# Value products of an attention stage: eight heads in two slots of a step in place of four heads in four

## The reference, cut to what matters

```python
scores = jnp.einsum('bhqd,bhkd->bhqk', q, k) / jnp.sqrt(jnp.asarray(D, q.dtype))
attn = jax.nn.softmax(scores, axis=-1)
out = jnp.einsum('bhqk,bhkd->bhqd', attn, v)
out = out.transpose(0, 2, 1, 3).reshape(B, N, C)
return out @ Wo.T + bo
```

## Time and profile before

| | |
|---|---|
| median of 3 runs | 976.9 us (973.17 to 978.64) |
| the profiled execution, its own time | 973.87 us |
| its span, first to last instruction | 972.1 us |
| TensorE busy with matmuls | 805.2 us, 83% |
| VectorE busy | 594.3 us, 61% |
| ScalarE busy | 404.9 us, 42% |
| GpSimd busy | 356.3 us, 37% |
| mean granted TensorE clock | 0.918 of full |
| L757 (value products) | 1024 records, 73.8 us busy |

### The profile page before, as it was taken

How to read it: one execution, slowest core, us unless ns; L and a number is a source line. 1 busy time by engine, 2 the same in 40 slices (tenths; PEclk the granted TensorE clock), 3 DMA queues, 4 the chain that set the end, 5 groups by cost and what they waited for, 6 DMA issues and landing times. The chain is left out here.

```text
span 972.1 us, 16867 instructions
## 1 busy us (share of the span) xinstructions
PE 805.2 (83%) x5933; PEld 635.1 (65%) x5933; DVE 594.3 (61%) x1410; ACT 404.9 (42%) x639; POOL 356.3 (37%) x290
## 2 busy tenths in 40 slices
PE   5999955568998888899888887885299999999993
PEld 4777734345666666666656665543299999999993
DVE  4879854444578776777877766643255555555542
ACT  4565621123555554455455545551243233423320
POOL 0333434212254444455354444223222344235422
PEclk9999988767999999999999999875599999999997
DMA  4116401553554454464455434100533332233100
GB/s 121 44 45 201 131 19 60 127 136 94 125 132 130 114 156 136 125 157 119 115 136 157 130 111 131 55 21 21 177 96 101 115 108 98 91 114 120 38 27 18
DMA packets 75913, 100.91 MB, mean 104 GB/s; under 512 B 10961, under 2 KB 63354, under 8 KB 75856
## 3 DMA queue, kind: packets, MB, share of 16 engines
q1 hardware_dynamic: 72400, 92.03, 34.0%
q0 software_dynamic: 3456, 8.13, 2.3%
HBM read 65.47 MB, written 35.74 MB: 104 GB/s over the span
## 5 line engine op out<-in xcount | busy, mean ns | idle before, releaser
L971 DVE TENSOR_REDUCE nmax<-ps_m 128x4 f32<-128x1024 f32 x128 | 156.7, 1224 | 117.5 <-PE ps_m L732 114.7
L925 ACT ACTIVATE pt<-ps_a 128x1024 f32<-128x1024 f32 x128 | 131.1, 1024 | 138.0 <-PE ps_a L742 136.6
L1238 ACT ACTIVATE hid<-ps_h 128x640 fp32r<-128x640 f32 x64 | 45.1, 705 | 151.3 <-PE ps_h L1178 151.3
L1178 PE MATMUL ps_h<-xt,w_hi 128*128 128x320 f32 x512 | 100.0, 318 | 1.0 <-DVE xt L1253 1.0
L732 PE MATMUL ps_m<-kst,qst 48*128 48x256 f32 x512 | 68.7, 349 | 33.7 <-DMA qst<-halves_dram 30.1
L732 PEld LDWEIGHTS ps_m<-kst,qst 48*128 48x128 f32 x512 | 41.2, 199 | 77.8 <-issue 35.6
L1287 DVE SCALAR_TENSOR_TENSOR hid<-ps_h,hid 128x640 fp32r<-128x640 f32 x64 | 52.8, 825 | 56.1 <-ACT hid L1238 55.6
L1190 PE MATMUL ps_y<-w_hi,hid 128*128 128x256 f32 x640 | 85.3, 284 | 1.7 <-issue 1.7
L1178 PEld LDWEIGHTS ps_h<-xt,w_hi 128*128 128x128 f32 x512 | 80.1, 191 | 5.5 <-DVE hid L1287 3.3
L1190 PEld LDWEIGHTS ps_y<-w_hi,hid 128*128 128x128 f32 x640 | 80.1, 191 | 1.9 <-issue 1.9
L166 POOL TENSOR_TENSOR gated<-xh,sgate 128x512 f32<-128x512 f32 x32 | 42.2, 1319 | 88.1 <-ACT xh L259 88.1
(11 more groups left out here) (169 smaller groups left out, 1623.9 us busy)
## 6 DMA issues: line engine op xcount, KB each, us to landing
halves_dram<-half SPq DMA_DIRECT2D x64, 256.0 KB, 2.5
gated<-in_w SPq DMA_DIRECT2D x16, 1024.0 KB, 5.5
kst<-halves_dram SPq DMA_DIRECT2D x64, 128.0 KB, 3.2
qst<-halves_dram SPq DMA_DIRECT2D x64, 128.0 KB, 3.2
rows_dram<-blank SPq DMA_DIRECT2D x1, 5160.0 KB, 19.2
gated<-rows_dram SPq DMA_DIRECT2D x8, 645.0 KB, 4.2
x_raw<-in_x_t SPq DMA_DIRECT2D x8, 512.0 KB, 3.8
xres<-in_x SPq DMA_DIRECT2D x16, 256.0 KB, 3.8
```

Source lines behind the costliest of these rows:

```text
L925: nc.scalar.activation(pt[:, k % 4].rearrange("p s t q -> p (s t q)"), ps_a[:].rearrange("p s t q -> p (s t q)"), ACT.Exp).then_inc(s["exp ...
L971: nc.vector.tensor_reduce(nmax[:, q, :, :, h // 2].rearrange("p t s -> p s t"), ps_m[:], AX.X, ALU.max, negate=True).then_inc(s["max_done" ...
L1178: mm = pe.matmul(ps_h[:, f % 2, c2, 0:HC], w1[a][:, p, k, f * P:(f + 1) * P], xt[:, b, p, k, c2 * HC:(c2 + 1) * HC], start=(n == 0 and k = ...
L1238: nc.scalar.activation(hid[:, HI, f, :].rearrange("p (c n) -> p c n", c=2), ps_h[:, f % 2, :, 0:HC], ACT.Relu).then_inc(s["hid_hi"], 1)
```

## The change

`weigh` is no longer called at h = 0 and h = 8. At h = 4 and h = 12 it is called twice, for groups g-1 and g: 16 matmuls in place of 8. The number of matmuls and their operands are the same. `pt` has one buffer for each of the 8 pairs of a batch, and ScalarE's wait ahead of an exponential names the value products of the same pair in the batch before.

```diff
-    pt = T("pt", [P, 4, 2, KT, S], F32)
+    pt = T("pt", [P, NP, 2, KT, S], F32)
...
-                                       pt[:, h // 2 % 4, h % 2, t, :],
+                                       pt[:, h // 2, h % 2, t, :],
...
-                    if head % PV == PV - 1 and on(n, lag):
+                    if head % (2 * PV) == 2 * PV - 1 and on(n, lag):
+                        weigh(j, p if lag == 2 else q, head // PV - 1)
                         weigh(j, p if lag == 2 else q, head // PV)
...
-                        need(act, s["pv_mm"], NG4 * j + k // 2 - 1)
-                        nc.scalar.activation(pt[:, k % 4].rearrange("p s t q -> p (s t q)"),
+                        need(act, s["pv_mm"], NG4 * j + k // 2 + 1 - NG4)
+                        nc.scalar.activation(pt[:, k].rearrange("p s t q -> p (s t q)"),
```

## The result

The changed kernel takes 1008.1 us in the median of 4 runs (1003.9 to 1012.0), the kernel before 975.0 (972.2 to 978.6): the ratio is 1.034, 95% interval 1.031 to 1.038. It is slower by 33 us, where 995 and at most 1004 had been forecast. The profiled execution took 1008.8 us, with a span of 1007.0 against 972.1.

A forecast was written before the change was run, and what follows sets the result against it. A chain passing between TensorE and VectorE was taken to bound the kernel. Loop 13.3, unrolled steps 2.0, ends 1 and 0, clock 3 made 19.3 us on 973.9: 993, or 995 for a median, range 981 to 1004.

The forecast's parts named there:

- What bounds the kernel: Loop step: a chain where TensorE sets the time at h = 4 and 10 to 14, VectorE around h = 0 and 8.
- What a group costs: At h = 4 and 12: a second group behind the first adds four rounds, 0.91 us.
- The cheap second group: Rival: at h = 4 and 12 the second group adds only 0.60 us, total 988; chance 0.17.
- h = 8: Group removed at h = 8: the second `sums_by_query` still waits for the first `onrm`, so only -0.16 us.
- h = 12: Group added at h = 12: no TensorE wait from there to `project_out`, so it counts whole, +0.91 us.
- The chain of a loop step: Sum for one loop step: 0.91 - 0.16 + 0.91 = +1.66 us; 13.3 us for steps 6 to 13.
- The clock: Longer idle at `keys`, h = 0: two more loop steps with a granted-clock dip at 1.8 us each, +3 us.
- steps 4 and 5: Unrolled full steps: VectorE's slack hides 0.57 of the 0.91 us at h = 4; 0.7 us each.
- The rival with dips everywhere: Rival: the clock dips in every loop step, 9 us in place of 3, 1001 or a little more; chance 0.13.
- The ends of the pipeline: Step 16 gains at h = 0 and 8, steps 17 and 18 lose at h = 4 and 12: together 0, uncertainty 2.
- The sum: Whole kernel: 13.3 + 2.0 + 1 + 0 + 3 = 19.3 us on the profiled execution's 973.9.
- The +1 that I gave step 3: Step 3: no `place_done` to wait for, +0.91 - 1.0 + 0.91, its h = 4 group at the low clock: +1.

The follow-up runs named there:

- the hole filled: The changed kernel with group 2 computed once more at h = 0, where it stood before: 993.4 us, ratio 1.016.
- the second profile: The changed kernel run and profiled again, with no edit: 1006.4 us, ratio 1.031.
- the tail apart: The changed kernel with groups 2 and 3 at their old places, h = 0 and 4, in steps 16 to 18 alone: 995.5 us, ratio 1.022.
- moving work into the wait: The kernel before with eight buffers, group 1 moved from h = 12 to h = 0 of the next step, ahead of group 2: 961.6 us, ratio 0.985.

## Why the prediction was wrong

- **What bounds the kernel: right at h = 0, 4 and 12.** Taking a group out at h = 0 gave nothing, `keys` only waits longer (2.72 us, 2.6 forecast), and a joined group costs its time at h = 4 and 12 and next to nothing at h = 0.
- **What a group costs: right.** 0.86 us measured, 0.91 forecast. The cheap second group (0.60) was not seen: the drain around the changed tiling mode, which is stated in the Trainium skill (TensorEngine Tiling (Array Packing), Key Properties), is worth no more here than the 2 x 1.00 - 1.87 = 0.13 us by which two groups apart exceed a joined one.
- **h = 8: right in cause, small in size.** -0.16 forecast. From `lg` to the second L769 it is 7.85 us in the even loop steps against 8.42 before, and 8.05 to 8.16 in the odd ones against 8.35: -0.2 to -0.6. The wait for `place_done` ahead of the first L769 is there (0.4 to 0.5 us), the wait of the second for `onrm` is not: in step 11 the first `onrm` ended at 500.62 + 0.42 = 501.04, 0.95 us before it. From `lg` to that end VectorE took 7.21 us where it had taken 8.21, which I had not foreseen (the tiny instructions of the last section). With groups 0 and 1 joined alone that time is not saved, and there the forecast holds to the letter: in step 6 the second L769 starts 0.06 us after the first `onrm` ends, and 8.26 us after `lg`.
- **h = 12: right** (+0.86 for 0.91). The chain of a loop step: 1.66 forecast, 1.3 to 1.7 by the full-clock steps with the hole filled and by the parts (0.86 - 0.45 + 0.86).
- **The clock: the step that failed first.** I took two more loop steps with a dip, 5 of 8; it was 8 of 8, and the unrolled steps 4 and 5 as well. That the loop came out right (13.3 + 3 = 16.3 forecast, 16.7 measured) is luck: with the dips that came, my prices give 13.3 + 9 = 22.3. Chain and dip together cost 2.7 us over a full-clock step of before, and I had priced them at 1.66 + 1.8. Steps 4 and 5 were given 1.4 us for their slack ahead of `lg` and cost 5.4 (6.6 in the second profile): VectorE idled 1.6 us ahead of `lg` there in the changed kernel, so the low clock had used up the slack that I counted on (0.5 and 1.9 us in the second profile). The rival with dips everywhere was the right one, and its 1001 was still too low, as it counted the loop alone.
- **The ends of the pipeline: the step that failed most.** Forecast 0 with an uncertainty of 2 for steps 16 to 18, and 0.3 for step 15; measured 9.0 together. I priced the removed group 2 of step 16 at the low clock from the earlier trace rows, as a gain, and the joined groups at the full one. It came the other way round: with group 2 gone, the joined groups at h = 4 ran wholly or mostly at the low level and took 3.3, 3.6 and 2.8 us in steps 16, 17 and 18. The run with the tail apart takes 11 to 13 us out of the total, 10 to 11 of them in that stretch, and so shows that the joining there is the cause. Why the low stretch falls where it does in step 16 stays open.
- **The sum.** 19.3 forecast on the profiled execution, 34.9 measured: 0.4 of the gap is the loop, 4.0 steps 4 and 5, 0.2 step 14, 8.7 step 15 and after, and 2.3 the time up to step 4. That last part is scatter: 4.6 us of the loss there lie before the first `r1`, ahead of any value product, and the second profile does not have them. The +1 that I gave step 3 did not show either (29.1 and 27.8 us in the two profiles, 29.4 before).

## What to carry to other kernels

Joining two pieces of work to save a switch is worth the switch (0.13 us here); where each piece stood is worth much more. Before work is taken out from behind a wait, look at what the clock does there: the piece may be cover that costs nothing and keeps TensorE's clock up. When the clock has fallen anyway, a piece at the front of the low stretch can spare the pieces on the critical chain behind it, but does not always: in step 16 it did so before the change and with the tail apart, and not with the hole filled. Price the ends of a pipeline by the clock that they will have after the change, and look for the opposite edit: moving work into the wait gained 14 to 15 us here.

## What the runs showed of the hardware

- More matmuls made the changed kernel faster: 128 useless ones at h = 0 took 13 to 15 us off it. 128 others at h = 8 added 18 to 20 us; in the loop most of that is the clock.
- In each of the eight loop steps of the kernel before, one of two tiny VectorE instructions behind `lg` takes 1.22 to 1.25 us: `slot` (L1042, a [128, 2] sum) in the even steps, `over` (L1041) in the odd ones. In the changed kernel both take 0.15 to 0.17 us in every step. In the kernel before the long one starts just behind an instruction of GpSimd (L609, from 508.93 in step 12 and from 480.67 in step 11); in step 11 of the changed kernel both have started when GpSimd starts at 500.30:

```profile
480.71 1.24 DVE L1041 TENSOR_SCALAR over<-place 128x2 f32<-128x2 f32 x1
...
509.00 1.23 DVE L1042 TENSOR_TENSOR slot<-slot,place 128x2 f32<-128x2 f32 x1
```

```profile
500.20 0.15 DVE L1043 TENSOR_TENSOR slot<-slot,place 128x2 f32<-128x2 f32 x1
```

  The shift in time took 1.1 us off VectorE's chain behind `lg`. That the overlap is the cause was not tested by itself.
